# Masking the attention scores with eight row-and-column tiles a token tile in place of two full-array matmuls

## The reference

```python
DEPTH, HEADS, DIM_HEAD, WINDOW = 6, 16, 64, 32
for i in range(DEPTH):
    x = attn_layer(shift_tokens(x), Wqkv[i], q_scale[i], k_scale[i], Wo[i]) + x
    x = ffn_layer(shift_tokens(x), ln_g[i], ln_b[i], W1[i], b1[i], W2[i], b2[i]) + x

# in attn_layer: q, k normalised, scaled and rotated, then local_attention:
#   windows of 32 queries; each sees the 32 keys of the window before and its own 32
mask = (it < jb) | (it > jb + w) | (jb == -1)      # jb == -1: no window before the first
sim = jnp.einsum('bhwie,bhwje->bhwij', bq, bk2) * QK_SCALE
sim = jnp.where(mask, -jnp.finfo(sim.dtype).max, sim)
attn = jax.nn.softmax(sim, -1)
out = jnp.einsum('bhwij,bhwje->bhwie', attn, bv2)
```

## Time and profile before

| | us |
|---|---|
| median of three runs | 3490.45 |
| lowest and highest of them | 3487.27, 3495.57 |
| span of the profiled execution | 3500.8 |
| TensorE busy (63036 matmul records) | 3344.2, 96% |
| TensorE weight loads | 2479.3, 71% |
| ScalarE busy | 2702.7, 77% |
| VectorE busy | 2441.7, 70% |
| GpSimd busy | 1445.3, 41% |

### The profile page before, as it was taken

One profiled execution on the slowest core, in us unless ns is written; L12 is line 12 of the kernel. 1 busy time (PEld: TensorE's weight loads), 2 busy tenths in 40 slices (PEclk: granted clock), 3 DMA queues, 4 the chain that ended last, 5 costly groups with the idle time before them and its releaser, 6 DMA issues.

```text
span 3500.8 us, 152322 instructions
## 1 busy us (share of the span) xinstructions
PE 3344.2 (96%) x63036; PEld 2479.3 (71%) x63228; DVE 2441.7 (70%) x5141; ACT 2702.7 (77%) x9033; POOL 1445.3 (41%) x1276
## 2 busy tenths in 40 slices
PE   6789999999999999999999999999999999999997
PEld 4457777677777767777767777767767767777775
DVE  5667777667777767777767777767767767777774
ACT  5667787768778777878777887868778787878876
POOL 2244444434444443444444444444444353444441
PEclk9899999999999999999999999999999999999998
DMA  2055656555655656565565566555555655565563
GB/s 71 1 115 122 140 122 129 121 123 120 143 123 123 132 118 134 127 130 126 112 138 118 127 135 131 120 130 117 127 129 121 133 129 127 117 130 126 116 135 76
DMA packets 361273, 421.42 MB, mean 120 GB/s; under 512 B 52291, under 2 KB 265814, under 8 KB 359814
## 3 DMA queue, kind: packets, MB, share of 16 engines
q1 hardware_dynamic: 360582, 411.67, 54.4%
HBM read 19.30 MB, written 2.10 MB: 6 GB/s over the span
## 4 chain that ended last, share of the span: by engine, by line
PE 69%; POOL 18%; issue 4%; DVE 2%; DMA 1%; ACT 1%; SPq 0%; POOLq 0%; DVEq 0%
PE ring_ps L1229 16%; POOL qs L612 12%; PE out_ps L1321 12%; PE out_ps L1331 9%; PE ring_ps L1274 8%; PE small_ps L1240 6%; PE score_ps L1292 4%; PE ring_ps L1303 4%; PE ring_ps L1367 4%; POOL probs L597 3%; DVE prod L988 2%; PE ring_ps L1264 2%; PE out_ps L1345 2%; PE score_ps L1284 1%; PE small_ps L1248 1%
## 5 line engine op out<-in xcount | busy, mean ns | idle before, releaser
L769 ACT ACTIVATE probs<-score_ps,neg_max,rq 128x64 f32<-128x64 f32 x3072 | 1194.7, 420 | 97.0 <-DVE neg_max L1026 95.7
L988 DVE TENSOR_TENSOR prod<-ring_ps,tables 128x512 f32<-128x512 f32 x1536 | 957.9, 681 | 292.4 <-PE ring_ps L1229 264.8
L612 POOL TENSOR_TENSOR ks<-prod 128x1024 f32<-128x1024 f32 x192 | 452.9, 2359 | 870.9 <-DVE prod L988 870.9
L1229 PE MATMUL ring_ps<-xs,wqk 128*128 128x256 f32 x3072 | 771.2, 389 | 17.2 <-issue 11.9
L769 ACT ACTIVATION_READ_ACCUMULATOR probs<-score_ps,neg_max,rq 128x1 f32 x3072 | 677.4, 221 | 0.0
L725 ACT ACTIVATE square<-ring_ps,biases 128x512 f32<-128x512 f32 x768 | 516.9, 687 | 200.9 <-DVE prod L988 199.1
L597 POOL TENSOR_TENSOR probs<-probs,inv_sums 128x512 f32<-128x512 f32 x384 | 401.0, 1044 | 608.8 <-DVE inv_sums L1040 608.7
L1229 PEld LDWEIGHTS ring_ps<-xs,wqk 128*128 128x128 f32 x3072 | 572.9, 192 | 107.3 <-issue 18.9
L612 POOL TENSOR_TENSOR qs<-prod 128x1024 f32<-128x1024 f32 x192 | 453.4, 2361 | 395.1 <-DVE prod L988 395.1
L1321 PEld LDWEIGHTS out_ps<-pt,v 64*64 64x64 f32 x24576 | 399.5, 136 | 119.2 <-issue 117.0
L758 ACT ACTIVATE att_t<-out_ps 128x512 f32<-128x512 f32 x384 | 217.0, 591 | 312.1 <-PE out_ps L1321 311.5
(11 more groups left out here) (182 smaller groups left out, 3809.4 us busy)
## 6 DMA issues: line engine op xcount, KB each, us to landing
v<-vs SPq DMA_DIRECT2D x1344, 128.0 KB
qt<-qs SPq DMA_DIRECT2D x768, 128.0 KB
kt<-ks SPq DMA_DIRECT2D x768, 128.0 KB
v<-vs SPq DMA_DIRECT2D x192, 64.0 KB
wqk<-in_L_ffn_Wqkv SPq DMA_DIRECT2D x6, 1024.0 KB, 5.2
wv<-in_L_ffn_Wqkv SPq DMA_DIRECT2D x6, 512.0 KB, 4.5
wo<-in_L_ffn_Wo SPq DMA_DIRECT2D x6, 512.0 KB
out_dram<-ks SPq DMA_DIRECT2D x16, 128.0 KB, 1.9
```

Source lines behind the costliest of these rows:

```text
L612: pool.tensor_tensor(dst, prod_a[p % 2], prod_b[p % 2], ALU.add).then_inc(rot_ready, 1)
L769: last = nc.scalar.activation(probs[i][:, j, e, :], score_ps[e][:, KEYS * j:KEYS * (j + 1)], ACT.Exp, bias=neg_max[:, h:h + 1], scale=rq[p ...
L988: last = V.tensor_tensor((prod_b if a else prod_a)[p % 2][:, f, :] .rearrange("p (u c) -> p u c", u=2), bank[:, :].rearrange("p (u c) -> p ...
L1229: last = mm(bank_of(s)[:, TOKENS * f:TOKENS * (f + 1)], wqk[:, n, 2 * c + f, a, :], xs[:, WINDOW:PADDED], start=True, stop=True)
```

## The change

A tile's mask goes in with eight matmuls. For window w (the 32 output partitions from 32 w) and parity e, the rows are the 64 partitions from 64 e, the weights the 64 x 32 part of the identity that picks the first 32 of them, and what is streamed are the 512 columns of the mask on those partitions. This is the shape of the score matmuls, and the same tiles of the array. The stored mask no longer has one entry a tile of tokens but one without and one with the missing window before; the second is used for tile 0, window 0. The wait for the queries' transfer (q_moved), which stood before the second mask matmul of tile 0, stands behind the masks.

```diff
@@ -1278,12 +1278,15 @@
                     i, half = s[1], s[2]
                     if half == 0:
                         pe.wait_ge(exp_ready, at(g, TILES * PARTS, PARTS * i))
-                        for e in range(2):
-                            if e == 1 and i == 0:
-                                pe.wait_ge(q_moved, moved(g, 1))
-                            mm(score_ps[e][:, :], ident_bf[:, :], mask_bf[:, i, :, :].rearrange("p j c -> p (j c)"),
-                               start=True, stop=False, skip_group_check=True)
+                        for w in range(WPT):
+                            kind_ = int(i == 0 and w == 0)
+                            for e in range(2):
+                                mm(score_ps[e][WINDOW * w:WINDOW * (w + 1), :],
+                                   ident_bf[64 * e:64 * e + 64, 64 * e:64 * e + WINDOW],
+                                   mask_bf[64 * e:64 * e + 64, kind_, :, :].rearrange("p j c -> p (j c)"),
+                                   start=True, stop=False, skip_group_check=True)
                     if i == 0 and half == 0:
+                        pe.wait_ge(q_moved, moved(g, 1))
                         pe.wait_ge(k_moved, moved(g, 1))
                     for j in range(PAIRS // 2 * half, PAIRS // 2 * (half + 1)):
                         for w in range(WPT):
@@ -1397,10 +1400,8 @@
     query = np.arange(P)[:, None] % WINDOW
     key = np.arange(KEYS)[None, :]
     hidden = (key > query + WINDOW) | (query > key)
-    mask = np.zeros((P, TILES, KEYS), np.float32)
-    for i in range(TILES):
-        no_window = (i == 0) & (np.arange(P)[:, None] < WINDOW) & (key < WINDOW)
-        mask[:, i] = np.where(hidden | no_window, MASKED, 0.0)
+    mask = np.stack([np.where(hidden | (first & (key < WINDOW)), MASKED, 0.0) for first in (False, True)], 1)
+    mask = mask.astype(np.float32)
```

## The result

| | us |
|---|---|
| before, in the same series (11 runs) | 3490.45 (3482.13 to 3498.58) |
| after (11 runs) | 3503.0 (3493.93 to 3513.68) |
| ratio | 1.0036, interval 1.0024 to 1.0048 |
| forecast | 3472, range 3451 to 3484 |
| profiled execution of after: span | 3503.7 |

The change makes the kernel slower by 0.36%, where 0.5% less was forecast. No rival held the cause.

The account below looks back on a forecast made before the run. TensorE was taken to bound the kernel except where GpSimd holds it before L1255. 96 x 0.20 = 19.2 us for the first tile, 0 for the second, less 1.2 for late keys: 3490.45 - 18.0 = 3472 us, range 3451 to 3484.

Parts of the forecast that it names:

- Part 3: Instructions of six more weight-load and matmul pairs a tile: priced at 0, or 0.07 us if they delay the scores.
- Parts 1 and 2: Ahead of the scores: shape change moved free, eight masks in one round; first score after 0.551 us against 0.74, gain 0.20.
- rival D: Score weights held until the masks of their own rows are through: gain only 0.11 us, 3480 us; chance 6%.
- Part 4: Moved wait for queries costs nothing, but earlier scores meet the keys' transfer earlier: 1.2 us lost in all.
- Part 5: Behind the first tile's scores, row maxima and square L777 leave 0.26 us of room, covering the 0.20 gain.
- Part 6: Second tile's 0.20 us is worth 0: TensorE waits for GpSimd before L1255, 0.13 us growing to about 0.33.
- the tie: At L1255, TensorE against GpSimd: TensorE already waits about 0.13 us in an ordinary batch, by the spacing of starts.
- B: First tile's scores are bound by instructions and masks relieve the queue: some 0.33 us gained in all, 3461 us; chance 10%.
- E: Two mask tiles in the same columns take turns: scores start at 0.76 against 0.74 us, 3492 us, no change; chance 10%.
- F: Long mask streams of different column tiles don't run side by side: slower, 3564 us at four rounds; chance 6%.
- C: Both tiles pay, GpSimd no longer holding TensorE before L1255: 38 us gained, 3452 us; chance 6%.

## Why the prediction was wrong

**Part 3 is the step that failed.** It priced six more pairs of weight load and matmul a tile at 0, because "instructions stand ready when the tiles begin". That looked at the row of 32 scores as a queue on the chip and took its refill for granted. But the instructions come by DMA, 256 at a time, and TensorE can be through a piece before the next is usable. In the place of the 0 the trace shows 28 us more of issue time before the scores. What the 24 instructions (with one wait more, 1342 for 1317) do is threefold, and no run parts the three: they put 272 in place of 260 into the densest stretch, they let more borders come by, and they change the step of the place from 37 to 62 a batch: 4 x 62 = 248, so every fourth batch stands only 8 from where the fourth before it stood, and a bad place comes back for many rounds. The page had the row of q8, and the view of waits had 5.0 us of issue in the scores in three pieces of up to 3.6. I read both past.

**The sum, step by step.** In the 72 ordinary batches that I could compare, after is 0.12 us shorter on average (33.50 and 33.45 in two traces of before, 33.38 and 33.32 in two of after), where 0.20 was forecast: 9 us gained; about 0.2 a batch where nothing is late, and part of it lost again at the borders. In the 21 batches around the changes of layer, after takes 10 to 12 us more (771.2 and 766.7 against 760.5 and 754.4). There the stalls in S00 are the longest: three of the five last batches of a layer take 34.5 to 36.6 us, with 1.8 to 2.2 of stall, where before has none over 33.6 at that point. Behind all these it takes 5 more, ahead of them 5 less. That these stalls are long because the weights of the next layer are then on the DMA queues is likely, but was only argued, and no run tests what other transfers do to the fetch. These sums account for the traces, whose spans stand 3 us apart in the first pair and 6 in the second. The medians stand 12.6 and 15.3 apart; the rest is in runs without a trace and is assigned to nothing.

**Parts 1 and 2** were right: 0.31 + 0.23 in place of 0.74, one round for eight masks. At places 76, 140 and 204 tile 0 gave 0.19 us a batch, forecast 0.20. The rule of the Trainium skill (TensorE: Matmul & The Clock Gate, Part 3) that speaks against the overlap of weight loads within a row group (rival D) is again not what the rows show: four masks share each half of the rows, yet the weight loads of all eight start within 0.02 us, those of the scores begin 0.03 after the first mask, while the masks stream, and the first score runs at 0.23. Read strictly, the rule would part the four masks of a half as well, which costs more than the 0.63 that rival D made of it.

**Part 4** misread its row. The 13 waits for keys are 12 idle times of the weight loads, 11 of them the 0.42 us that the first load of the scores has behind nearly every mask, and a single wait of a matmul, 1.1 us. What counts is how late the first score follows the masks: before, 1 batch is late, by 1.2 us; after, 10 batches, by 3.4 us in all. So the term was 2.2 us by these traces and 0.8 by the second pair, forecast 1.2: the size is right by luck. **Part 5** was right: the square (L777) starts 0.417 us after the second record of the centring matmul in both kernels. **Part 6** was right in its mechanism, the idle time of TensorE before L1255 grew by 61.7 - 41.6 = 20 us, 0.21 a batch (in the view of lines, before and then after); and tile 1 brought nothing at places 76, 140 and 204. The 105 waits of the earlier trace rows count weight loads too; the tie itself came from the distances between starts, and those held.

```profile
L1255 PE MATMUL ring_ps<-ident_bf,rk_bf 128*48 128x128 bf16 x192 | 28.7, 233 | 41.6 <-POOL rk_bf L591 37.1
```
```profile
L1255 PE MATMUL ring_ps<-ident_bf,rk_bf 128*48 128x128 bf16 x192 | 28.7, 233 | 61.7 <-POOL rk_bf L591 61.5
```

**The rivals.** B had the right resource and the wrong sign: it saw the instructions as a queue that the masks would help to fill. D, E and F argued about the array, and the array did as forecast. C wanted both tiles to pay, and the growing wait before TU speaks against it.

## What to carry to other kernels

An instruction is not free where many short ones stand together: here 256 of them had to last about 4 us, in one kernel 5.5, and a stretch that uses them up much faster pays up to 2 us when a border falls late into it. Count the instructions that an edit adds to such a stretch before pricing its work, look for "issue" in the view of the waits and for the row of instruction packets, and prefer a form that does the same work with no instruction more: two masks of 64 rows and 128 columns gave 12 us where eight masks lost as much. A time that changes by 0.2 to 0.7% may be the borders' alone: shift the kernel by a few instructions before believing in a cause.

## What the runs showed of the hardware

- TensorE's instructions are fetched while the kernel runs, 16 KB a packet, 509 packets in after. The Trainium skill (Trainium Architecture — The Big Picture, The software stack) has the instruction streams moved into each engine at load time; the trace disagrees.
- A packet starts mostly 0 to 2.8 us after the border before it is passed, takes 0.9 to 1.7 us, and the instructions at a stalled border of S00 run 2.2 us or more after its start. In after two packets start at least 3.35 us apart.
- 18 instructions ahead of 96 unchanged batches moved the time by 23 us.
- 66 instructions of two waits already met lengthened the step WO by 3.3 us, 50 ns each (91 of them by 6.0 us, 66 ns each, at a mean clock of 0.933); in the kernel with new masks and 1408 instructions, single increments, one or two ahead of a matmul of 0.2 us or one ahead of 0.1 us, lengthened no step by more than 0.06. In the one with old masks, two ahead of each turn of 0.1 us lengthened T10 by about 0.4.
- A change of tile shape cost 0.09 us once more between masks of 64 x 128 and scores of 64 x 32.
